# First cross-attention's keys and values projected in the state-space loop and streamed back from DRAM, with their stores issued by ScalarE

## The reference, cut to what matters

```python
x = x + _L0_attn_ref(_layernorm(x), W_in, dw_kernel, ..., W_out)      # state-space block
x = x + _L0_xattn_ref(_layernorm(x), ctx, ctx, mask, wq, bq, wk, bk, wv, bv, wo, bo)
```

## Time and profile before

| | |
|---|---|
| median of 3 runs (lowest to highest) | 2842.92 us (2836.62 to 2844.7) |
| the profiled execution, its own time | 2844.52 us |
| span of its instructions | 2842.7 us |
| mean granted TensorE clock | 0.909 of full |
| busy: TensorE, VectorE, ScalarE, GpSimd | 2446.9, 1947.9, 1565.1, 461.1 us |
| DMA moved | 168.10 MB, mean 59 GB/s |

### The profile page before, as it was taken

How to read it: one execution, slowest core, us unless ns; L and a number is a source line. 1 busy time by engine, 2 the same in 40 slices (tenths; PEclk the granted TensorE clock), 3 DMA queues, 4 the chain that set the end, 5 groups by cost and what they waited for, 6 DMA issues and landing times. The chain is left out here.

```text
span 2842.7 us, 59554 instructions
## 1 busy us (share of the span) xinstructions
PE 2446.9 (86%) x20502; PEld 1684.8 (59%) x20503; DVE 1947.9 (69%) x4438; ACT 1565.1 (55%) x3006; POOL 461.1 (16%) x494
## 2 busy tenths in 40 slices
PE   7767877746899999999886899999999899969993
PEld 3333434323566676766674477777776555559993
DVE  2699999996577777777665477777777455662224
ACT  2666666651466666666373466666666233305553
POOL 0010000003100000000031211111110133224551
PEclk9878888867899999999886899999999799969997
DMA  4476666763000000000001000000000310002225
GB/s 110 104 160 158 157 159 156 157 156 76 17 22 16 22 16 22 16 22 11 1 16 40 8 23 22 22 22 22 22 22 6 114 32 16 17 22 65 70 70 177
DMA packets 84698, 168.10 MB, mean 59 GB/s; under 512 B 11040, under 2 KB 65730, under 8 KB 84354
## 3 DMA queue, kind: packets, MB, share of 16 engines
q0 software_dynamic: 15264, 75.25, 12.4%
q1 hardware_dynamic: 69330, 91.50, 10.9%
HBM read 92.17 MB, written 15.83 MB: 38 GB/s over the span
## 5 line engine op out<-in xcount | busy, mean ns | idle before, releaser
L1249 DVE CUSTOM_DVE_ANT_0 xa_h_scores<-xa_h_score_bank,xa_h_added 112x375 f32<-112x375 f32 x1024 | 518.1, 544 | 150.2 <-PE xa_h_score_bank L1184 127.5
L1343 ACT ACTIVATE xa_h_probs<-xa_h_scores,xa_h_negmax 112x375 f32<-112x375 f32 x1024 | 561.4, 600 | 0.9 <-DVE xa_h_negmax L1256 0.6
L1196 PEld LDWEIGHTS xa_h_turn_bank<-keep_ident,xa_h_probs 112*125 112x125 f32 x3072 | 396.1, 189 | 91.7 <-DVE xa_h_probs_t L1263 23.1
L1196 PE MATMUL xa_h_turn_bank<-keep_ident,xa_h_probs 112*125 112x112 f32 x3072 | 435.9, 278 | 9.3 <-DVE xa_h_probs_t L1263 9.1
L1263 DVE COPY xa_h_probs_t<-xa_h_turn_bank 125x448 f32<-125x448 f32 x512 | 319.1, 623 | 148.4 <-PE xa_h_turn_bank L1196 134.9
L1349 ACT ACTIVATE xa_h_probs_t<-xa_h_turn_bank 125x448 f32<-125x448 f32 x256 | 138.6, 541 | 301.1 <-PE xa_h_turn_bank L1196 301.0
L615 DVE TENSOR_TENSOR_SCAN mb_state<-mb_decay,mb_drive 128x1792 f32<-128x1792 f32 x64 | 248.5, 3883 | 0.8 <-ACT mb_decay L551 0.4
L1184 PE MATMUL xa_h_score_bank<-xa_h_keys,xa_h_queries 32*112 32x375 f32 x2048 | 231.6, 522 | 10.7 <-DVE xa_h_row_max L1249 10.0
L1209 PEld LDWEIGHTS xa_h_sums_bank<-xa_h_probs_t,xa_h_values 125*32 125x32 f32 x6144 | 141.1, 110 | 154.1 <-DVE xa_h_probs_t L1263 149.0
L423 PE MATMUL mb_front_bank<-mb_normed_t,mb_w_eff 128*128 128x448 f32 x512 | 207.9, 567 | 19.0 <-ACT mb_normed_t L508 18.4
L1209 PE MATMUL xa_h_sums_bank<-xa_h_probs_t,xa_h_values 125*32 125x112 f32 x6144 | 201.4, 264 | 14.5 <-issue 6.6
(11 more groups left out here) (354 smaller groups left out, 3864.9 us busy)
## 6 DMA issues: line engine op xcount, KB each, us to landing
mb_y<-mb_read_out POOLq DMA_DIRECT2D x64, 896.0 KB, 6.9
mb_rows<-mb_low_rows SPq DMA_DIRECT2D x64, 448.0 KB, 4.1
xa_context<-in_ctx_t SPq DMA_DIRECT2D x64, 375.0 KB, 3.1
lm_w<-in_m_w SPq DMA_DIRECT2D x16, 512.0 KB, 10.3
lm_e_wide<-lm_result_rows SPq DMA_DIRECT2D x8, 896.0 KB, 9.0
keep_x<-in_x SPq DMA_DIRECT2D x4, 896.0 KB, 15.6
lm_latent_rows<-lm_rows SPq DMA_DIRECT2D x8, 448.0 KB, 3.2
out_x<-keep_x SPq DMA_DIRECT2D x8, 448.0 KB, 6.1
```

The source lines that it names most:

```text
L1196: last = pe.transpose(turn_bank[(par + kc) % 2][0:KP, g * S:(g + 1) * S], probs[par][:, g, kc * KP:(kc + 1) * KP], keep.ident[0:S, 0:S])
L1249: dve.tensor_tensor_reduce(scores[par][:, g, :], score_bank[g][0:S, 0:SK], added[s][:, :], 1.0, -BIG, ALU.add, ALU.max, row_max[par][:, g: ...
L1343: act.activation(probs[par][:, g, :], scores[par][:, g, :], ACT.Exp, bias=negmax[s][:, G * c + g:G * c + g + 1]).then_inc(probs_ready, 1)
```

## The change

`KeysAndValues` holds two DRAM tensors, keys of 128 x 750 words for each batch and values of 125 x 816 words (with a column of ones). In each group of the state-space loop TensorE now projects the keys and values of the group's four batches (`keys_and_values`) into four PSUM banks of their own, ScalarE reads them (`read_keys_and_values`) and issues the two stores itself (`store_keys_and_values`); SyncE loads the contexts into one buffer. The rows of B and C are now two DMAs of 224 KB into two slots each, instead of one into four. In the first cross-attention `project` for keys and values, their reads and the context loads are gone; SyncE loads stored keys and values two batches ahead. The second cross-attention still projects. The stationary operand of the weighing is 17 columns wide in the first cross-attention instead of 32.

```diff
+            def keys_and_values(t):
+                wk, wv = ahead.weights.wk, ahead.weights.wv
+                pe.wait_ge(context_in, 16 * (t + 1))
+                for m in range(DC):
+                    reuse(pe, kv_read, KV_PARTS * (t - 1) + m + 1)
+                    for c in range(DC):
+                        last = pe.matmul(kv_bank[m][:, 0:SK], wk[:, c, m * 128:(m + 1) * 128], context[:, c, :], start=c == 0, stop=c == DC - 1)
+                    last.then_inc(kv_done, 1)
+                for part, chunks in ((2, (0, 1)), (3, (2,))):
...
@@ TensorE, group(g, k, at, final)
+                    if n == 1:
+                        keys_and_values(G * g)
+                    if n == 3:
+                        keys_and_values(G * g + 1)
+                    if n == 4:
+                        keys_and_values(G * g + 2)
                     if n == 5:
                         if not final:
                             low_rank(g)
                         project_out(g, 1 - k, 0) if not first else pass_over(OUT_A)
+                    if n == 6:
+                        if not final:
+                            deltas(g)
+                        keys_and_values(G * g + 3)
@@ ScalarE
+            def read_keys_and_values(t):
...
+                        act.activation(keys_out[:, m, :], kv_bank[m][:, 0:SK], ACT.Identity, bias=bk[:, m:m + 1]).then_inc(kv_read, 1)
...
+                store_keys_and_values(t)
+            def store_keys_and_values(t):
+                act.wait_ge(kv_read, KV_PARTS * t + 2)
+                act.sem_inc(kv_store_started, 1)
+                act.dma_start(ahead.keys[bass.ds(t, 1)].rearrange("o p c k -> (o p) (c k)"), keys_out[:, :, :].rearrange("p c k -> p (c k)")
...
                     if n == 2:
-                        read_inner(g, (0, 1))
+                        if not final:
+                            read_inner(g, (0, 1))
+                        read_keys_and_values(G * g)
+                    if n == 3:
+                        if not final and at != GROUPS - 2:
+                            normalise_rows(g + 2)
+                        read_keys_and_values(G * g + 1)
+                    if n == 4 and not final:
                         read_inner(g, (2, 3))
+                    if n == 5:
+                        read_keys_and_values(G * g + 2)
+                    if n == 6 and not final:
                         softplus(g)
                     if n == 7:
+                        read_keys_and_values(G * g + 3)
+                    if n == 7 and not final:
                         decays(g + 1, 0)
                         decays(g + 1, 1)
@@ SyncE, group
+                    if n == 0 and at != 0:
+                        load_context(G * g)
+                    if n == 3:
+                        load_context(G * g + 1)
+                    if n == 5:
+                        load_context(G * g + 2)
+                    if n == 6:
+                        load_context(G * g + 3)
@@ attention_heads
-                    if has(t + 1):
+                    if has(t + 1) and projected:
                         project(t, s, ("keys0", "keys1", "values01", "values2")[c])
+            def load_keys_and_values(t, s):
+                sp.wait_ge(scores_done, NQ * (t - 1))
+                sp.dma_start(keys[s][:, :, :], stored.keys[bass.ds(t, 1)].rearrange("o p c k -> (o p) c k")).then_inc(keys_in[s], 16)
+                sp.wait_ge(weighed, NQ * (t - 1))
+                sp.dma_start(values[s][:, :, :, :], stored.values[bass.ds(t, 1)].rearrange("o p c h v -> (o p) c h v")).then_inc(values_in[s], 16)
```

More of the change, by code:

```diff
@@ L1017, in attention_heads @@
         queries = [sb(f"queries{n}", [128, DC, 2, S]) for n in range(2)]
-        keys = [sb(f"keys{n}", [128, DC, SK]) for n in range(2)]
-        values = [sb(f"values{n}", [KP, KC, H, VP]) for n in range(2)]
+        if projected:
+            context, context_in = source
+            keys = [sb(f"keys{n}", [128, DC, SK]) for n in range(2)]
+            values = [sb(f"values{n}", [KP, KC, H, VP]) for n in range(2)]
+        else:
+            keys, values, keys_in, values_in = source
         scores = [sb(f"scores{n}", [S, G, SK]) for n in range(2)]
@@ L1063, in place @@
             if isinstance(t, int) and t == 0:
-                return 4 + [p for p in PLACES if p != "sums"].index(what)
-            before = 4 + len(PLACES) - 1
+                return 4 * projected + [p for p in PLACES if p != "sums"].index(what)
+            before = 4 * projected + len(PLACES) - 1
             if isinstance(t, int) and t >= B - 1:
@@ L1150, in project @@
             def project(t, s, what):
[L1152 removed]
+                reuse(pe, proj_read, place(t, what))
                 if what == "masked_values":
+                    if not projected:
+                        pe.wait_ge(values_in[s], 8 * (t - s) + 16)
                     for kc in range(KC):
```

148 lines of the change are left out of this document (105 added, 43 removed).

## The result

| kernel | median, us | lowest to highest | runs | ratio to before, 95% interval |
|---|---|---|---|---|
| before | 2841.93 | 2836.62 to 2844.70 | 4 | |
| after | 2883.31 | 2870.74 to 2889.15 | 4 | 1.0141 [1.0118, 1.0164] |

The change makes the kernel 1.4% slower, clear of the noise. It was forecast at 2833 us with a range of 2798 to 2868: both wrong. The profiled execution is the fastest of the four of after (2870.74 us, 26 above the profiled one of before), so its rows show less of the loss than the medians, 41 us, do.

A forecast was written before the change was run, and what follows sets the result against it. It took the loop as bound by VectorE, with two operations close behind TensorE's chain, and the heads by a circle of scores and maxima. 56 - 53 - 12.5 = -9.5 us from 2844.5, less 1.6 to the median, gave 2833, range 2798 to 2868.

The forecast's parts named there:

- Loop: DMA: State-space loop: the added key, value and context transfers, at most 21 us of all engines a group, cost 0.
- Projections in the loop, +56: State-space loop: projections delay the low rank product and its followers, 8 us in each of 7 groups, 56 us.
- the rival in which the loop hides them: State-space loop: unseen slack absorbs the low rank product's lateness, loop costs 0 to 28 us, 2792 to 2806 us; chance 0.17.
- the one of +81 us by the clock: State-space loop: clock not given back, or ScalarE's issues dear; 11.5 us a group, 81 us, total 2858 us; chance 0.16.
- ScalarE's issues, 0.37 us each: State-space loop: each DMA issue by ScalarE costs near SyncE's price, 0.37 us, two issues for a batch's stores.
- The rows of state 6 may come 1 to 2 us late, inside the 5.3 us that VectorE waits anyway: SyncE's queue in the loop: state 6 rows wait behind `load_context`, 1 to 2 us late, within VectorE's existing 5.3 us wait.
- The rival with the accumulation chain, 2889 us, 0.09: GpSimd's DMA in the loop: added traffic makes each accumulation cost 10.4 us, loop +112 us, total 2889 us; chance 0.09.
- Heads, -53: First cross-attention's heads: 31 batches without projections save 1.71 us each, 53 us.
- The circle: Heads: VectorE's maxima from four score banks, TensorE's next scores, then maxima again bound the batch; removing projections saves 1.71 us.
- Start of the heads, -12.5: Start of the heads: batch 0's 13.5 us of projections go, about 1 us of waiting for spread queries stays; 12.5 us saved.

The follow-up runs named there:

- experiment 11: Changed kernel with values as 128 rows, and the stores of keys and values issued by SyncE instead of ScalarE: 2843.63 us.
- experiment 2: Changed kernel with the projections kept but one context load and one pair of stores in all; every batch uses batch 0's keys and values: 2837.79 us.
- Experiments 4: Changed kernel with the context loads issued from ScalarE's queue instead of SyncE's: 2894.48 us.
- 6: Changed kernel (125 rows) with all context loads but only batch 0's stores: 2837.74 us.
- experiment 3: Changed kernel with all context loads and stores but no projection matmuls and no reads of their banks; stores write constants: 2868.12 us.
- stores only: Changed kernel (125 rows) with all stores of keys and values but only one context load, of batch 0: 2862.47 us.
- Experiment 10: Changed kernel with values as 128 rows, and the second third of the transposes issued twice in the first cross-attention: 2863.02 us.
- experiment 1: Kernel before with only the B and C rows split into two transfers and two slots each: 2832.65 us.
- 5: Changed kernel with the values stored and loaded as 128 rows instead of 125, the three added rows unused: 2851.18 us.
- 9: Changed kernel with values as 128 rows, batches 2 and 3 projected later in the group and their contexts loaded later: 2862.38 us.
- 14: Changed kernel with 128 rows and SyncE's stores, B and C rows again one transfer in four slots, and a single drive buffer: 2852.11 us.

## Why the prediction was wrong, point by point

*The step that failed* is "Loop: DMA", with its "I take 0". It measured 81.5 - 56.2 = 25.3 us of the loop in the profiled executions, and by medians, over the whole kernel, 2883.3 - 2837.8 = 45.5 us; ScalarE's issues, some 8 us of it (experiment 11), are in both. It was not the bytes: the DMA share of the loop is 0.79 where the prediction reckoned with 0.90. The term watched one wait only, VectorE's for the accumulations, and let each grow to 9.6 us. It grew to 8.9 + 0.9 = 9.8, and VectorE waited 5.6 us for it; the rest came by the other waits. The prediction had both halves of the reason on the page and dropped them: the 6.3 to 10.5 us to landing, and the sentence on five engines, which it used for a rival's chance alone. The table that the runs make (the second column is arithmetic):

| rows of the values | largest divisor up to 16 | median, us | loop, us |
|---|---|---|---|
| 128 | 16 | 2851.2 | 611.2 |
| 126 | 14 | 2860.1 | 618.1 |
| 125 | 5 | 2883.3 | 626.3 |
| 127 | 1 | 3591.6 | 961.2 |

The time follows the divisor, not the number of rows or bytes. By the Trainium skill (DMA: Bandwidth & Descriptors, "Why a DMA increments its semaphore by 16 and not by 1") the largest number up to 16 that divides the rows is the number of engines that a DMA uses. These four runs agree with it in their order; no view here shows the engines one by one, so the mechanism is inferred. With 128 rows instead of 125 the median is 32 of the 41 us lower. Two ways are open by which the rows act, and no run separates them (a second buffer for the values' stores would): accumulations and B rows of the same time take 8.9 and 5.1 us with 125 rows against 7.6 and 4.5 with 128, and ScalarE waits 21.6 us for its own store against none. With 127 rows the second clearly leads.

*The other rule that was weighed* (the Trainium skill, DMA: Bandwidth & Descriptors, "Issuing engines are not separate DMA queues") adds that issuing from several engines saves only the time of the issue, usually small beside the DMA itself. Experiment 11 shows that this time counts on an engine that others wait for: 7.9 us of the loop.

*Projections in the loop, +56*: right, within the 6 us for issues that the term held and experiment 2 doesn't have. 56.2 us, with the waits of `add_to_x` and `make_delta` in their places (experiment 2). The clock came back as assumed, 0.91 over the loop in that kernel. Nothing supports the rival in which the loop hides them (its own terms give 2777 to 2805 us, not 2792 to 2806), nor the one of +81 us by the clock; that the loop of after grew by 81.5 us, at a clock of 0.90, is a coincidence. In after a group lasts some 80 us, not 76 to 78.

*ScalarE's issues, 0.37 us each*: the shortest of the values' are 0.29 us, but twelve of the 32 took between 0.49 and 1.46 us.

*"The rows of state 6 may come 1 to 2 us late, inside the 5.3 us that VectorE waits anyway"*: right in place, too small in size. Seven of the 13 waits are at state 6, 2.1 to 4.8 us each and 23.0 of the 36.2 us. Experiments 4 and 6 show that such a wait largely stands in for another.

*The rival with the accumulation chain, 2889 us, 0.09*: nearest in time (2883.3), by a mechanism that is only partly its own. Its chain shows bare in experiment 3 (62 us), where no projection slows VectorE. In after VectorE waits just 5.6 us for it, in stores only 14.0, in groups already stretched by the projections. Its +112 us in the loop were 81.5.

*Heads, -53*: measured -36.2. The circle was read rightly: the 15 batches of 31 at the full clock take 18.3 us (maxima at 879.8 and 898.2 us) against the 18.2 forecast. Missing is what no row of before could show, since the clock is 1.00 in its heads: with the projections gone TensorE is busy 486 of 580 us instead of 601 of 620, and in three stretches of the stage the granted clock falls. The batch from 1142.7 to 1162.7 us takes 20.0 us at a mean clock of 0.93, where the one at 1.00 takes 18.4. Over the 15 batches in which it falls that is some 14 us. Experiment 10 held the clock with repeated transposes and gained nothing.

*Start of the heads, -12.5*: measured -6.0. Without the traffic it is 775.6 - 703.5 = 72.1 us from last scan to first maximum, 14.3 less than before: here too the transfers' term was most of what was missing. Some of it is spread: the kernel of experiment 1 has 82.8 us there instead of 86.4 with nothing changed.

*The sum*, by profiled executions: 81.5 - 6.0 - 36.2 = +39.3, where the forecast had 56 - 12.5 - 53 = -9.5. Of the 48.8 us between, 25.5 are the loop's transfers, 6.5 the start, 16.8 the heads (14 of them the clock).

*What stays open*: by which wait the 125 rows act, and why every arrangement of the projections (2, 5, 9, 11, 14) leaves a loop of 600 to 620 us. The waits move between the output projection, softplus, decays and B rows; a version that spreads the work over more than one group's steps wasn't tried. The best one with the change (experiment 11) only equals before; the kernel with the rows split, which needs no change in the heads, is 0.4% below it, though not by its loop.

## What to carry to other kernels

Before moving a transfer into a busy stage, look at the number of its rows, not only at its bytes: three unused rows made 128 of 125 and gave back three quarters of the loss. In a loop where three engines and two queues meet at every step, a wait in the profile names who came last, and not what the time costs; remove one suspect at a time and compare the length of the loop. When work leaves a stage that was bound by something else, reckon with the clock that the emptier engine is granted.

## What was not expected of the hardware

- A store of 127 rows beside these accumulations holds ScalarE up to 30.0 us; with 128 rows it never waits.
- One issue of a DMA by ScalarE takes from 0.29 to 1.46 us in the same loop, at the same line.
- TensorE's granted clock in the heads fell from 1.00 to 0.97 in the mean when it had less to do: busy 97% of the time in before's window, 84% in after's. With the repeated transposes of experiment 10, busy 89%, it was 1.00 again. In the loop the same change raised it from 0.80 to 0.90.
